# Where the biases of the strong experts are added in the first expert pass: products on TensorE, or additions on VectorE in PSUM

## The reference

```
h   = x @ W_in + b_in                                  # 128 -> 256
agg = segment_sum(h[src], dst) / max(indegree, 1)
logits = [h, agg] @ router_W + router_b; top 2 of 8; gates = softmax of the two
weak_e   = relu(agg @ weak_W[e] + weak_b[e])           # 4 experts, 256 -> 256
sh_e     = relu(agg @ strong_W1[e] + strong_b1[e])     # 4 experts, 256 -> 512
strong_e = sh_e @ strong_W2[e] + strong_b2[e]          # 512 -> 256
h = h + sigmoid(h @ conf_W + conf_b) * sum_e gate_e * expert_e
```

## Time and profile before

| | before |
|---|---|
| median of three runs | 6586.23 us |
| the profiled execution | 6593.85 us |
| its span, from first to last instruction | 6592.1 us |
| TensorE busy, share of the span | 91% |
| VectorE busy | 62% |
| ScalarE busy | 39% |
| mean granted clock of TensorE | 0.884 |
| first expert pass | about 1056 to 2172 us |

### The profile page before, as it was taken

How to read it: one execution, slowest core, us unless ns; L and a number is a source line. 1 busy time by engine, 2 the same in 40 slices (tenths; PEclk the granted TensorE clock), 3 DMA queues, 4 the chain that set the end, 5 groups by cost and what they waited for, 6 DMA issues and landing times. The chain is left out here.

```text
span 6592.1 us, 134329 instructions
## 1 busy us (share of the span) xinstructions
PE 5968.8 (91%) x44527; PEld 4773.7 (72%) x44527; DVE 4115.6 (62%) x11478; ACT 2587.2 (39%) x6535; POOL 2523.9 (38%) x2576
## 2 busy tenths in 40 slices
PE   3999996999999799999989999978888887999999
PEld 1555554777777688888778888865666665989998
DVE  6777763666666466666546666657777776555544
ACT  3555542333433233333234444432322233554444
POOL 0000000000000577777567777747777774000000
PEclk6999997999999899999999999985555555999999
DMA  5444346555553666666566666645555555777776
GB/s 144 137 127 134 102 134 210 175 191 176 178 171 129 181 186 187 186 186 186 150 191 192 193 192 189 192 124 146 148 148 148 150 148 158 255 239 248 246 262 224
DMA packets 745651, 1163.76 MB, mean 177 GB/s; under 512 B 247969, under 2 KB 571077, under 8 KB 742914
## 3 DMA queue, kind: packets, MB, share of 16 engines
q1 hardware_dynamic: 550786, 590.39, 28.8%
q0 software_dynamic: 147392, 438.33, 24.0%
q10 hardware_dynamic: 46784, 126.44, 5.4%
HBM read 982.50 MB, written 172.42 MB: 175 GB/s over the span
## 5 line engine op out<-in xcount | busy, mean ns | idle before, releaser
L571 POOL DMA_INDIRECT ring<-parts,src_idx x1664 | 1625.2, 977 | 651.0 <-issue 473.1
L571 POOL DMA_INDIRECT ring<-rows_yh,src_idx x832 | 831.3, 999 | 319.7 <-issue 238.6
L2722 PE MATMUL agg_ps<-worked,halved 128*128 128x448 f32 x4060 | 864.1, 370 | 10.0 <-DVE halved L2948 8.3
L2722 PEld LDWEIGHTS agg_ps<-worked,halved 128*128 128x128 f32 x4060 | 758.7, 189 | 72.7 <-issue 8.5
L1218 PEld LDWEIGHTS hid<-agg,big 128*128 128x128 f32 x6272 | 740.6, 192 | 40.7 <-issue 36.2
L1218 PE MATMUL hid<-agg,big 128*128 128x128 f32 x6272 | 757.4, 276 | 0.0
L1109 ACT ACTIVATE strong<-hid,s_b 128x128 f32<-128x128 f32 x1568 | 447.8, 369 | 640.6 <-PE hid L1218 636.5
L2866 ACT CAST worked<-acc 128x1344 fp32r<-128x1344 f16 x294 | 385.9, 1313 | 376.5 <-PE agg_ps L2722 346.6
L2957 DVE CAST worked<-acc 128x1792 fp32r<-128x1792 f16 x294 | 320.9, 1094 | 300.0 <-PE agg_ps L2722 291.1
L693 DVE TENSOR_TENSOR acc<-acc,sums 128x128 f32 x416 | 120.2, 289 | 576.0 <-PE sums L723 455.8
L735 PE MATMUL zt<-ywin,onehot_t 64*128 64x128 bf16 x2496 | 364.1, 304 | 115.1 <-DMA ring<-rows_yh,src_idx 101.1
(11 more groups left out here) (457 smaller groups left out, 10965.8 us busy)
## 6 DMA issues: line engine op xcount, KB each, us to landing
acc<-adj SPq DMA_DIRECT2D x392, 784.0 KB, 5.2
rows_ring<-halves SPq DMA_DIRECT2D x98, 896.0 KB
adj<-big ACTq DMA_DIRECT2D x7, 5488.0 KB
adj<-acc ACTq DMA_DIRECT2D x7, 5488.0 KB
relb<-rel_rows ACTq DMA_DIRECT2D x106, 256.0 KB, 4.3
ring<-parts,src_idx POOLq DMA_INDIRECT x1664
parts<-cut SPq DMA_DIRECT2D x98, 192.0 KB, 1.9
hp<-parts SPq DMA_DIRECT2D x98, 192.0 KB
```

Of the source, the lines that this page charges most:

```text
L571: nc.gpsimd.indirect_dma_start(ring[:, k, 0:YH] if edge_net else ring[:, k, :], None, table, bass.IndirectOffsetOnAxis(ap=src_idx[:, i * R ...
L2722: ins = nc.tensor.matmul(ps[:, 0:HALF_COLS], rows_in[:, c, k * per + s, :], sheet[:, s * HALF_COLS:(s + 1) * HALF_COLS], start=(k == first ...
```

## The change

TensorE no longer multiplies the second biases in a block. Each up group is then one f32 product per column group, which starts and stops the accumulation itself. VectorE makes a second mask, `has_all` (128 partitions by 128 nodes, ones and zeros), behind `agg`, and after each group of up products adds the bias in place: for each of four column groups PSUM = mask * bias of the partition + PSUM (`based0` to `based3`, four instructions each). ScalarE's ReLU waits for `basedN` as well. `on_dve`, which Layer1In took from Layer1, is written out for it: based0 at place 6, behind the gates; based1 behind the four down biases; based2 behind the first strong term; based3 behind the second. In the fold the second biases of the strong experts are now multiplied straight into columns (sixteen records of one column for each expert in place of four of 512), and one copy of 128 x 4 takes the place of the five instructions of `cut_rows`.

```diff
-            S1_AT, WEAK_AT, ROUTER_AT = 0, NW * 2 * H, NW * 3 * H
+            WEAK_AT, ROUTER_AT = 0, NW * H
-            DVE = ROUTE + "down_b0 down_b1 down_b2 down_b3 mix0 mix1 mix2 mix3 mix4 mix5"
+            DVE = (ROUTE + "based0 down_b0 down_b1 down_b2 down_b3 based1 mix0 mix1 mix2 mix3 mix4 based2 mix5 based3")
...
                 def biases(n):
                     if n >= 2:
                         pe.wait_ge(self.sem["fold_dve"], n)
-                    for a in range(2):
+                    for j in range(4 if n >= 2 else 0):
+                        for a in range(2):
+                            ins = nc.tensor.matmul(p["y"][:, n % 2, j:j + 1], self.raw(n, a)[:, j * P:(j + 1) * P],
+                                                   w["turned_in"][:, 2 + a, 0:1], start=(a == 0), stop=(a == 1))
+                    for a in range(2 if n < 2 else 0):
...
-                    cut_rows(p["y"][0:PARTS, n % 2, :], (self.WEAK_AT if n < 2 else self.S1_AT - 4 * H) + n * 2 * H)
+                    if n < 2:
+                        cut_rows(p["y"][0:PARTS, n % 2, :], self.WEAK_AT + n * 2 * H)
+                    else:
+                        nc.vector.tensor_copy(s["s1_has"][:, n - 2, :], p["y"][:, n % 2, 0:4]).then_inc(self.sem["fold_dve"], 1)
...
             def aggregate(self, m, b):
...
+                m.need_before(self.dve, "based3")
+                nc.vector.tensor_scalar(s["has_all"][:, :], s["rdeg"][:, :], 0.0, None, ALU.is_gt)
...
             def up(self, m, e):
...
                 for j in range(4):
-                    at = self.S1_AT + e * 2 * H + j * P
-                    nc.tensor.matmul(p["hid"][:, bank_at, j * P:(j + 1) * P], s["bias"][:, at:at + P], s["has"][:, :],
-                                     start=(j == 0), stop=False, skip_group_check=True)
+                    ins = nc.tensor.matmul(p["hid"][:, bank_at, j * P:(j + 1) * P], w["s1_in"][:, e, j * P:(j + 1) * P],
+                                           s["agg"][:, :], start=True, stop=True)
+                m.done(f"up{e}", ins)
...
+            def based(self, m, e):
+                s, p = self.b
+                m.need(self.pe, f"up{e}")
+                if e == 0:
+                    m.need(self.dve, "has_edges")
+                bank_at = (2, 0, 1, 2)[e]
                 for j in range(4):
...
+                    hid = p["hid"][:, bank_at, j * P:(j + 1) * P]
+                    ins = nc.vector.scalar_tensor_tensor(out=hid, in0=s["has_all"][:, :], scalar=s["s1_has"][:, e, j:j + 1],
+                                                         in1=hid, op0=ALU.mult, op1=ALU.add)
+                m.done(f"based{e}", ins)
+
+            def relu_strong(self, m, e):
+                m.need(self.dve, f"based{e}")
+                super().relu_strong(m, e)
```

More of the change, by code:

```diff
@@ L1348, in buffers @@
                       ("g2", [P, NE]), ("gate", [P, NE]), ("row", [P, H]), ("left", [P, H]), ("above0", [PARTS, 1]),
-                      ("above1", [PARTS, 1]))}
+                      ("above1", [PARTS, 1]), ("has_all", [P, P]), ("s1_has", [P, NW, 4]))}
                 at = NW * H
@@ L1514, in up @@
                 for j in range(4):
-                    at = self.S1_AT + e * 2 * H + j * P
-                    nc.tensor.matmul(p["hid"][:, bank_at, j * P:(j + 1) * P], s["bias"][:, at:at + P], s["has"][:, :],
-                                     start=(j == 0), stop=False, skip_group_check=True)
-                for j in range(4):
-                    ins = nc.tensor.matmul(p["hid"][:, bank_at, j * P:(j + 1) * P], w["s1_in"][:, e, j * P:(j + 1) * P],
-                                           s["agg"][:, :], start=False, stop=True, skip_group_check=True)
@@ L1521, in up @@
-                m.done(f"up{e}", ins)
+                    ins = nc.tensor.matmul(p["hid"][:, bank_at, j * P:(j + 1) * P], w["s1_in"][:, e, j * P:(j + 1) * P],
[7 more added lines that the diff above has]
+                bank_at = (2, 0, 1, 2)[e]
+                for j in range(4):
+                    hid = p["hid"][:, bank_at, j * P:(j + 1) * P]
+                    ins = nc.vector.scalar_tensor_tensor(out=hid, in0=s["has_all"][:, :], scalar=s["s1_has"][:, e, j:j + 1],
+                                                         in1=hid, op0=ALU.mult, op1=ALU.add)
+                m.done(f"based{e}", ins)
@@ new lines, in relu_strong, with on_dve @@
+            def relu_strong(self, m, e):
+                m.need(self.dve, f"based{e}")
+                super().relu_strong(m, e)
+            def on_dve(self, dve, m, i, b, added):
+                s, p = self.b
+                row = s["row"][:, :]
+                yield from self.route_dve(dve, m, b, added)
+                yield 6
+                self.based(m, 0)
+                yield 7
+                dve.wait_ge(self.sem["block_out"], i * 32 + 16)
+                for e in range(NW):
+                    self.mix(m, f"down_b{e}", row, self.w["down_b"][:, e, :], NW + e, row if e else s["h"][:, :])
+                self.based(m, 1)
+                m.need(self.act, "relu_w0")
+                self.mix(m, "mix0", row, s["weak"][:, 0, :], 0, row)
+                self.mix(m, "mix1", row, s["weak"][:, 1, :], 1, row)
+                yield 8
+                m.need(self.act, "relu_w1")
+                self.mix(m, "mix2", row, s["weak"][:, 2, :], 2, row)
+                self.mix(m, "mix3", row, s["weak"][:, 3, :], 3, row)
+                yield 10
+                m.need(self.pe, "down0")
+                self.mix(m, "mix4", row, p["y"][:, 0, 0:H], NW, row)
+                self.based(m, 2)
+                yield 13
+                m.need(self.pe, "down1")
+                self.mix(m, "mix5", row, p["y"][:, 1, 0:H], NW + 1, row)
+                self.based(m, 3)
```

## The result

The changed kernel took 6620.5 us (median of five, 6619.45 to 6625.99) against 6586.33 before (five, 6578.67 to 6594.8): a ratio of 1.0052, 95% interval 1.0041 to 1.0064. It is slower by half a per cent, and the forecast was 6612. The profiled execution took 6622.01 us (span 6620.2), 28 us more than that of before.

The account below looks back on a forecast made before the run. TensorE, busy 994.41 of 995 us, was taken as the bound. Loop 8, tail 10, fold 0 and clock 8 sum to 26 us on the 6586.23 median: 6612 us; own range 6600 to 6630, overall 6566 to 6665.

Parts of the forecast that it names:

- 0.51 us saved a group: TensorE's up groups: dropping four bias products saves 0.51 us each, 2.04 us a block, 100 us over 49 blocks.
- Rival D: TensorE's up groups: only 0.41 or 0.32 us saved per group, 10 to 20 us on top, about 6628; chance 0.10.
- 1.15 us a group of additions: VectorE, after each up group: four additions of 128 columns in PSUM take 1.15 us.
- Rival B: VectorE's additions: a group takes 0.92 us, making an even exchange, about 6583 us; chance 0.22.
- rival C: VectorE's additions: writing to PSUM is dear, 2.0 us per group, about 6714 us, half way 6660; chance 0.12.
- 5.9 us to the first down product, and 11.1 us of waits there in seven blocks: First down product starts 5.9 us after the logits; TensorE waits there 11.1 us per seven blocks, against 14.3 saved.
- Rival A: TensorE stays the bound: 98 to 100 us saved, 10 lost in the tail, about 6500 us; chance 0.16.
- 4.4 us of later waits: Behind the first down product, per seven blocks: waits for group three and for VectorE's and ScalarE's conversions, together 4.4 us.
- The 0.8 for group three: Group three's additions are late for TensorE's down product in two of seven blocks, by 0.3 and 0.5 us.
- The tail, 2.6 us a block: Four blocks without counted products: 4.7 us of waits for 2.04 saved, 2.6 us a block, 10 us.
- The fold, nothing: Fold at the start: sixteen one-column records replace four for each of four matrices, 1.9 us against 1.9; nothing, within 2 us.
- The clock, five falls at 1.6: TensorE's granted clock falls after new waits: five falls at 1.6 us, 8 us; none would be 0, all sixteen 26.

Follow-up runs that it names:

- the filled kernel: Changed kernel with unread products put on TensorE ahead of the wait for the first ReLU, in the longest-wait blocks and the last four: 6602.5 us.
- additions and products together: Changed kernel with the 16 bias products of a block kept beside VectorE's additions: 6648.9 us, ratio to before 1.0089 to 1.0120.
- the mixed kernel: Against the changed kernel: first group's additions inside the gate chain, second group's bias by products, fourth group's additions one place later: 6539.5 us.
- the last kernel: The mixed kernel with the third ReLU one place later, behind ScalarE's conversion of counts: 6527.4 us, ratio to before 0.9899 to 0.9926.

## Why the prediction was right, step by step

- **0.51 us saved a group.** From five counted products to the next over an up group now pass 1270.02 - 1268.12 = 1.90 us, against 2.44. Without any bias a block is 2.06 us shorter; 2.04 was forecast. Rival D, by which a group of products gave back only 0.32 to 0.41, falls.
- **1.15 us a group of additions.** 1.13 measured; an addition lasts 0.351 and they start 0.26 apart. Rival B (0.92) and rival C (2.0) fall with it. The Trainium skill (Perfetto Trace Analysis, Optimizing Scalar/DVE Operations), which gives an access to PSUM about twice the price of one to SBUF, spoke for C. The lengths don't show it, for writes either: an addition of 128 columns in PSUM lasted 351 ns, and the same operation from SBUF, 485 for 256 columns, would come to 357 for 128 at the forecast's 1 ns a column (an estimate). In the starts a difference may lie, since these additions are 0.26 apart and the `agg` of 128 columns from SBUF is followed after 0.21; but that is another operation, and no run here takes the two apart. The forecast had the 0.26 in its sum already.
- **5.9 us to the first down product, and 11.1 us of waits there in seven blocks.** 5.86 and 11.1 measured. By the gaps the seven waits read 0.72, 1.78, 0.73, 1.57, 2.36, 1.38 and 1.58, together 10.1; but a record that ends ahead of a gap lasts longer than the next one's start needs (1.05 against 0.89 for four counted products), and by the starts of the same records in the kernel without the bias each wait costs 0.10 to 0.17 more. Without the bias TensorE is there 5.0 us after the logits in the blocks with the long cover and 4.2 to 4.4 in the others; 5.0 and 4.2 were forecast. Rival A, which wanted the ReLU in time, falls, although its 6500 is what TensorE can do: 6493 without the additions.
- **4.4 us of later waits.** 2.2 by the gaps (ScalarE's conversion 0.39 and 0.95, VectorE's conversion behind group four 0.87), 3.0 from start to start. VectorE's conversion was right (1.1 forecast and measured). For ScalarE's the two blocks were right, the 1.6 and 0.9 were not: 0.7 and 1.2. The 0.8 for group three did not come; the third and fourth down products cost 0.6 in two blocks of seven, and the fourth was not in the forecast.
- **The tail, 2.6 us a block.** 3.15, and 2.5 with the waits filled (19.4 against 16.9): the size of the waits was right, the difference is the clock.
- **The fold, nothing.** From its first transposes to the first logits 56.4 us, against 57.1 before.
- **The clock, five falls at 1.6.** Nine. The price was right in the loop: from the first of the eight down records behind the wait to the record after them pass 3.40 us (1362.52 to 1365.92), against 1.72 in the kernel without the bias (1329.11 to 1330.83), 1.7 more. In the tail a fall cost about 1.0 (20.3 and 20.4 us a block with it, 19.4 without). Together nearly 13 us where 8 were forecast; the count was the mis-sized term.

Sum by the profiles: 15.0 in the loop, 4 x 3.15 = 12.6 in the tail, -0.7 in the fold, 26.9 us with the clock in both, against 26 forecast. The rest of the 28 lies outside the change. That the sum is so near is in part luck. With the falls counted by themselves it reads 5.0 in the loop (15.0 less six falls at 1.67; 8 forecast), 9.9 in the tail (four blocks of the filled kernel; 10), -0.7 in the fold (0) and 12.7 for the clock (8): the forecast had the loop 3 us too dear and the clock 5 too cheap, and the two cancel in part.

The medians lie 34 us apart because the profiled execution of before was 7.5 us above its median and that of the changed kernel 1.5. The fold began anywhere from 1044 to 1055 us in the profiles, in stages that no edit touches, so some us of any one comparison are nobody's.

Against the kernel without the bias, the changed kernel's period is 16.75 us longer. TensorE's row is the same in the two, and the starts of its records, compared one by one over the second period, place all of it: 11.1 at the first down products, 0.3 in the products just behind four of them, 1.7 in the down records at the low clock, 3.0 at the later waits, 0.6 at the third and fourth down products.

## What to carry to other kernels

An engine with 38% free time is not free at the point where a chain passes through it: before work goes there, follow the chain from its latest input to its consumer and compare its length with what the consumer has to do meanwhile. If the chain is longer, either put the work ahead of the late input (here the gates) or leave just as much on the full engine as it would have waited. A step of a chain that is used several times in a block can be worth several times its length, and a new wait on TensorE can cost its clock on top.

## What was not expected of the hardware

How long a wait lowers the clock isn't sharp in these traces. In the changed kernel all six waits of 2.4 us and three of the four of 3.4 brought 0.50, the seven of 1.8 to 2.0 never did. But with additions and products together only one of four waits of 2.37 us brought it, and in the filled kernel one of seven of 1.8 to 2.0. In the last blocks of the mixed kernel two of four waits of 1.78 us brought it, and none of the four of 1.78 us at the same places of the last kernel. So the length of a wait alone doesn't decide it here. Each of these falls lasted 3.4 us.

VectorE's price for one instruction of 512 columns (755 ns) against four of 128 (1.13 us) is 0.37 us less. From the start of one to that of the next pass 0.26 us for 128 columns and 0.66 for 512: by these two some 1.04 ns a column and 0.125 us for each instruction (an estimate), so that in a chain the number of instructions counts beside the columns. That holds although VectorE had time to spare: the joined additions won their time as length of the chain.
